# Attention inner order: a later values-and-sums block, earlier normalising, and Wo loaded in four pieces

## The chip, the cores and the metric

The kernel runs on one core of one Trainium2 chip. The metric is the device time in microseconds, the median of the runs; lower is better.

## The reference

A gated cross-attention block (16 batches, 100 queries, 361 keys, width 512, 16 query heads in 4 groups that share keys and values) followed by a gated feed-forward block with weights quantised to three levels and activations to 8 bits.

```python
scores = einsum('bqghd,bkgd->bghqk', Q / sqrt(dh), K) + m * rel   # ALiBi slope times distance
scores = where(mask, scores, neg)
w = softmax(scores, axis=-1)
out = einsum('bghqk,bkgd->bqghd', w, V).reshape(b, q_len, 512)
return out @ Wo
...
x = x + tanh(g_xattn) * xattn(layernorm(x), ctx, ctx, mask, Wq, Wk, Wv, Wo)
x = x + tanh(g_ffn) * ffn(layernorm(x))      # silu(bit_linear) * bit_linear, rms_norm, bit_linear
```

## The kernel before

The program is written engine by engine, with its own semaphores: each engine's order is the order of its code. There are four stages: normalising x and projecting Q (kept in a scratch in DRAM), projecting K and V of the 16 batches, attention, and the feed-forward block over 12 full tiles of 128 rows and a tail. POOL quantises the feed-forward weights (24 pieces of 1024 columns, L526 to L538) during attention, each piece waiting for the loads that free its place; ring buffers of queries and keys (`qs`, `ks`, four slots) are filled from DRAM by SP.

Attention runs in steps b; one step works on three batches at once. A step on PE has eight slots u. Slot u begins with `scores(b, u)` (L1340): the plain scores of two heads of batch b, written to `wide[u % 2]`, from which DVE takes the row maxima (`largest_scores`, L1005). Behind them comes what the table `BEHIND[u]` lists, each entry with how many batches it lags:

- `("t", lag, j)`: `scores_t`, block j of 12 of the transposed scores (L1354), to `bank[j % 2]`; ACT takes its exponential into `p_t` (L718). Block 0 needs the batch's stored maxima (`nm_in`).
- `("pv", lag, kt)`: `values_and_sums`, one of three blocks (L1364, L1367): four matmuls of values and four of row sums, twice four rows of the trace, into `bank[2]` and `bank[3]`. After the third, ACT copies both out (`keep_pv`: `sum_kept` L731, `o_t` L732), and the next batch's first block waits for that.
- `("turn", ...)`: the maxima of the last batch are turned (L1373), copied by ACT to `nm_t` (L724, in the trace under its helper's line L631), and stored by SP into the rows of `qs` (`store_max`, L391). Slot 1's scores wait for the copy.

`scores(b, u)` also waits for the maxima of two slots before (u - 2), since they share a buffer. So slot 3 waits for the maxima of slot 1, slot 6 for those of slot 4, and slot 0 of the next step for those of slot 6.

The sums of a batch are inverted by ACT (`log_sums` L739, `inverse_sums` L744) in the step after the copy, between the exponentials of blocks 5 and 6. DVE refines the inverse and multiplies (`normalise(b - 3, step)`, steps 0, 1 and 2: L1021, L1024, L1029). The table `NORMALISE_BEHIND` says behind which slot's maxima each of them stands.

Wo is 1 MB. SP loads it (L432), ACT copies it at reduced precision to `wo_h` (L811, under L631 in the trace) behind step 9, and DVE forms `wo_l` (L1062) behind step 10. It is used after the last step. SP's order within a step is: `store_max(b - 1)`, then `load_qk(b + 2)` (L399, L401, L406) once transposed block 11 of batch b - 2 is done, then Wo.

Of the kernel before, what the change touches and what calls it, by code (L numbers as in the profile page):

```python
# [36 lines left out]
B, SQ, D = 16, 100, 512  # L37
# [3 lines left out]
G, HPG, DH = 4, 4, 32  # L41
# [33 lines left out]
QUANT_BYTES = QCH * 2  # L75


NORMALISE_BEHIND = {3: (0, 1), 5: (2,)}
O_TILES = (2, 3, 4, B)
BEHIND = {0: [("t", 2, 4), ("t", 2, 5), ("pv", 2, 0), ("turn", 1, 0), ("t", 2, 6), ("t", 2, 7)],  # L80
          1: [("t", 2, 8)],
          2: [("t", 2, 9), ("t", 2, 10)],
          3: [("t", 2, 11), ("pv", 2, 1)],
          4: [("t", 1, 0)],
          5: [("t", 1, 1), ("t", 1, 2), ("pv", 2, 2)],
          6: [("t", 1, 3)],
          7: []}


def flamingo_block(nc, x, ctx_t, mask, gates, wq, wk, wv, wo, w_ffn, ln_w, alibi_q, alibi_k, eye, out):  # L90
# [143 lines left out]
    with ctx:  # L234
# [3 lines left out]
        def sem(name):  # L238
            return ctx.enter_context(nc.semaphore(name))
# [9 lines left out]
        wo_in = sem("wo_in")  # L249
# [94 lines left out]
        def _(sp):  # L344
# [42 lines left out]
            def store_max(b):  # L387

                sp.wait_ge(nm_ready, b + 1)
                for part in range(2):  # L390
                    sp.dma_start(qs[b % SLOTS][ROWS_S + part:ROWS_S + part + 1, :, :].bitcast(F32).rearrange("p g (h q) -> p (g h) q", h=HPG),  # L391
                                 nm_t[H * part:H * part + H, :].bitcast(F32)).then_inc(nm_in, 16)

            def load_qk(b):

                slot = b % SLOTS
                q, n = q_scratch[b:b + 1], "o t (d g) n -> (o t d) g n"
                for rows, src in ((qs[slot][0:2 * DH], q), (qs[slot][2 * DH:3 * DH], q[:, 0:1])):
                    sp.dma_start(rows.bitcast(F32), src.rearrange(n, g=G)).then_inc(qk_in[slot], 16)  # L399
                for third, part in enumerate((0, 0, 1)):  # L400
                    sp.dma_start(ks[slot][DH * third:DH * (third + 1)].bitcast(F32),  # L401
                                 k_all[:, b, part, :].bitcast(F32)).then_inc(qk_in[slot], 16)
                if b == LATE_SLOT:
                    store_max(1)
                    sp.wait_ge(late_set, 2)
                sp.dma_start(ks[slot][100:101, :, 0:SK].bitcast(F32),  # L406
                             m_scratch[b:b + 1].rearrange("(o g) n -> o g n", g=1).broadcast_to([1, G, SK])).then_inc(qk_in[slot], 16)
# [13 lines left out]
            def attention_step(b):  # L421
                if b == 1:
                    store_max(0)
                    sp.wait_ge(kl_ready, B)
                    load_qk(LATE_SLOT)
                elif b > 2:
                    store_max(b - 1)
                if 2 <= b < B - 2:
                    sp.wait_ge(st_done, (b - 1) * UNITS)
                    load_qk(b + 2)  # L430
                if b == 8:
                    sp.dma_start(wo_f[:, :, :], wo).then_inc(wo_in, 16)  # L432

            def load_xb(t, par, rows=P):
                if not (isinstance(t, int) and t < 2):
# [193 lines left out]
        def _(act):  # L629
# [82 lines left out]
            def exps(b, *units):  # L712

                for j in units:
                    act.wait_ge(st_done, b * UNITS + (j + 1))
                    if j % G == 0 and b > 0:
                        act.wait_ge(pv_done, b * 3 - (2 - j // G))
                    nc.scalar.activation(p_t[:, j, :], bank[j % 2][0:KT, 0:HQ], ACT.Exp).then_inc(exp_done, 1)  # L718
# [16 lines left out]
            def log_sums(b):  # L735
                act.wait_ge(o_copied, b * 2 + 1)
                if not (isinstance(b, int) and b == 0):
                    act.wait_ge(o_ready, b)
                nc.scalar.activation(log_sum[:, :], sum_kept[:, :], ACT.Ln).then_inc(log_ready, 1)  # L739
# [38 lines left out]
            def attention_step(b):  # L778
                if b >= 2:
                    exps(b - 2, 4, 5)  # L780
                if b >= 3:
                    log_sums(b - 3)
                    inverse_sums(b - 3)
                if 2 <= b <= B:
                    turned_max(b - 1)
                if b == B + 1:
                    xq_round(0)
                if b >= 2:
                    exps(b - 2, 6, 7)
                if b == B:  # L790
                    o_high(1)
                if b == B + 1:
                    first_out()
                if b >= 2:
                    exps(b - 2, 8, 9, 10, 11)
                if b <= B:
                    exps(b - 1, 0, 1, 2)
                if 2 <= b <= B:
                    keep_pv(b - 2)
                if b <= B:  # L800
                    exps(b - 1, 3)

            for b in range(B):
                ctx_step(b)
# [2 lines left out]
            for b in range(1, STEPS):  # L807
                attention_step(b)
                if b == 9:
                    act.wait_ge(wo_in, 16)  # L810
                    copy_high(wo_h[:, :, :], wo_f[:, :, :]).then_inc(wo_high, 1)  # L811
                if b == B - 2:
                    act.wait_ge(wo_low, 1)
                    o_high(0)
# [87 lines left out]
        def _(dve):  # L902
# [150 lines left out]
            for b in range(2, B):  # L1053
                for u in range(PAIRS):
                    largest_scores(b, u)
                    if b >= 3:
                        for step in NORMALISE_BEHIND.get(u, ()):
                            normalise(b - 3, step)
# [529 lines left out]
```

## Time and profile before

| | |
|---|---|
| median of 3 runs | 531.79 us (531.22 to 534.74) |
| the profiled execution | 530.64 us |
| its span, first to last instruction | 528.8 us |
| PE busy, DVE busy, ACT busy, POOL busy | 89%, 70%, 62%, 44% of the span |
| chain that ended last, by engine | PE 51%, ACT 14%, DVE 14%, DMA 11%, issue 6% |
| step 2 of attention begins | 153.15 us |
| step 15 of attention begins | 312.61 us |
| mean granted TensorE clock | 0.982 |

The share of busy time is an average over stages. A matmul's end is modelled and matmuls overlap, so the distance between starts says more than their durations. A row of windows has the stretch, its length, the busy time and count of instructions of PE, PE's weight loads, DVE, ACT and POOL, the granted clock (1.00 is 2.4 GHz), the DMA engines' busy share and GB/s. The chain that ended last is followed back from the last instruction to what released each piece of work.

### The profile page before, as it was taken

How to read it: one execution, taken by the hardware profiler on the slowest of the kernel's cores; microseconds unless marked ns; L12 is line 12 of the kernel's file. 1: busy time of each engine (PE TensorE's matmuls, PEld its weight loads, DVE VectorE, ACT ScalarE, POOL GpSimd, SP SyncE). 2: the span in 40 equal slices, each digit the busy share in tenths (PEclk: the TensorE clock that was granted, in tenths of full speed). 3: DMA queues.
4: the chain of work that ended last, by engine and by line, in shares of the span. 5: the costliest groups of instructions: out<-in, count | busy, mean ns of one | idle time of the engine just before them, and what ended most of it. 6: DMA issues, size and time to landing. Idle time of an engine off the chain costs nothing.

```text
span 528.8 us, 8322 instructions
## 1 busy us (share of the span) xinstructions
PE 472.7 (89%) x2854; PEld 296.5 (56%) x2854; DVE 368.5 (70%) x674; ACT 327.9 (62%) x560; POOL 232.8 (44%) x250
## 2 busy tenths in 40 slices
PE   1799979998989999988889999888999999999965
PEld 1699979987954444443444445434454555555522
DVE  4876634466646888885698785387777777777762
ACT  2366637566336666664766776667777777777760
POOL 1000000000156677855263680147777677777630
PEclk9999999999979999998999999999999999999998
DMA  7889897999548788879667730112534333333323
GB/s 196 244 276 401 323 363 251 245 349 283 151 89 205 177 191 196 198 156 246 146 135 169 161 107 32 71 31 40 135 86 91 89 89 89 89 90 89 70 51 70
DMA packets 62402, 85.51 MB, mean 162 GB/s; under 512 B 37314, under 2 KB 48786, under 8 KB 60446
## 3 DMA queue, kind: packets, MB, share of 16 engines
q1 hardware_dynamic: 57182, 59.87, 44.5%
q0 software_dynamic: 3456, 12.58, 8.8%
q10 hardware_dynamic: 1728, 12.58, 6.8%
q8 instruction: 21, 0.34, 0.3%
q14 instruction: 15, 0.12, 0.1%
HBM read 57.94 MB, written 9.85 MB: 128 GB/s over the span
## 4 chain that ended last, share of the span: by engine, by line
PE 51%; ACT 14%; DVE 14%; DMA 11%; issue 6%; SPq 2%; POOL 1%; ACTq 0%; POOLq 0%; DVEq 0%
PE bank L1364 7%; DMA ct<-ctx_t 6%; PE bank L1354 6%; PE wide L1340 6%; PE wide L1271 6%; PE bank L1367 6%; PE wide L1440 5%; PE bank L1271 5%; PE bank L1312 5%; PE bank L1450 3%; ACT p_t L718 3%; DVE row_max L1005 3%; ACT sq_junk L832 2%; ACT act L822 2%; DMA qs<-nm_t 2%
## 5 line engine op out<-in xcount | busy, mean ns | idle before, releaser
L1005 DVE TENSOR_REDUCE row_max<-wide 100x2 f32<-100x722 f32 x128 | 110.4, 902 | 36.4 <-PE wide L1340 36.2
L718 ACT ACTIVATE p_t<-bank 121x400 f32<-121x400 f32 x192 | 92.4, 503 | 52.5 <-PE bank L1354 48.7
L1440 PE MATMUL wide<-w_q,xq 128*128 128x512 bf16 x384 | 86.8, 380 | 2.7 <-DVE h L1122 2.4
L572 POOL TENSOR_TENSOR z<-h,lnw 128x512 f32<-128x512 f32 x48 | 61.0, 1272 | 15.3 <-DVE h L1122 14.7
L1440 PEld LDWEIGHTS wide<-w_q,xq 128*128 128x128 bf16 x384 | 35.5, 98 | 51.6 <-DVE h L1122 7.9
L526 POOL DMA_DIRECT2D quant_in<-w_ffn x24 | 14.3, 595 | 99.5 <-PE bank L1312 93.0
L1340 PE MATMUL wide<-ks,qs 101*100 101x362 f32 x192 | 49.6, 346 | 9.0 <-DVE row_max L1005 5.2
L1354 PE MATMUL bank<-qs,ks 103*121 103x400 f32 x144 | 51.1, 386 | 6.1 <-DMA qs<-nm_t 2.5
L1312 PE MATMUL bank<-wv_f,ct 128*121 128x128 f32 x384 | 46.2, 278 | 4.3 <-DMA ct<-ctx_t 4.3
L952 DVE TENSOR_TENSOR ctl<-ct,cth 128x1445 fp32r<-128x1445 f32 x16 | 26.6, 1664 | 31.8 <-ACT cth L631 31.8
L1312 PEld LDWEIGHTS bank<-wv_f,ct 128*121 128x121 f32 x384 | 45.4, 189 | 4.9 <-DMA ct<-ctx_t 4.9
L840 ACT ACTIVATE z<-z,small 128x1024 f32<-128x1024 f32 x24 | 29.6, 1235 | 29.4 <-DVE small L1156 29.4
L1450 PE MATMUL bank<-w_q,yq 128*128 128x512 bf16 x192 | 45.3, 390 | 2.3 <-DMA yq<-y_int 2.3
L538 POOL TENSOR_SCALAR w_q<-quant_in 128x1024 bf16<-128x1024 f32 x24 | 31.9, 1329 | 34.4 <-DMA ks<-m_scratch 26.8
L1340 PEld LDWEIGHTS wide<-ks,qs 101*100 101x100 f32 x192 | 28.5, 168 | 29.2 <-issue 16.9
L1122 DVE TENSOR_TENSOR h<-act,wide 128x512 f32<-128x512 f32 x50 | 34.2, 685 | 13.8 <-ACT act L822 13.5
L1364 PE MATMUL bank<-p_t,v_all 120*32 120x400 f32 (+1 forms) x384 | 43.6, 526 | 0.0
L1367 PE MATMUL bank<-p_t,ones_keys 120*32 120x400 f32 (+1 forms) x384 | 42.2, 512 | 0.0
L822 ACT ACTIVATE act<-wide,small 128x512 f32<-128x512 f32 x50 | 33.6, 676 | 7.9 <-PE wide L1440 7.7
L1354 PEld LDWEIGHTS bank<-qs,ks 103*121 103x121 f32 x144 | 25.8, 188 | 18.1 <-ACT p_t L718 11.7
L531 POOL TENSOR_SCALAR quant_in<-quant_in,small 128x1024 f32<-128x1024 f32 x24 | 28.4, 1184 | 16.6 <-DMA quant_in<-w_ffn 14.3
L1450 PEld LDWEIGHTS bank<-w_q,yq 128*128 128x128 bf16 x192 | 18.7, 99 | 26.9 <-DMA yq<-y_int 4.3
(157 smaller groups left out, 919.3 us busy)
## 6 DMA issues: line engine op xcount, KB each, us to landing
quant_in<-w_ffn POOLq DMA_DIRECT2D x24, 512.0 KB, 5.7
ct<-ctx_t SPq DMA_DIRECT2D x16, 722.0 KB, 10.3
ks<-k_all SPq DMA_DIRECT2D x36, 181.0 KB
q_scratch<-qhl SPq DMA_DIRECT2D x16, 400.0 KB, 7.5
abs_a<-w_ffn ACTq DMA_DIRECT2D x6, 1024.0 KB, 7.2
abs_b<-w_ffn ACTq DMA_DIRECT2D x6, 1024.0 KB, 9.0
qs<-q_scratch SPq DMA_DIRECT2D x12, 400.0 KB
xb<-x SPq DMA_DIRECT2D x12, 256.0 KB, 2.9
```

What stands on the lines that cost most here:

```text
L572: nc.gpsimd.tensor_tensor(z[par][0:rows, c], h[0:rows, c], lnw[0:rows, c], ALU.mult).then_inc(z_done, 1)
L718: nc.scalar.activation(p_t[:, j, :], bank[j % 2][0:KT, 0:HQ], ACT.Exp).then_inc(exp_done, 1)
L822: nc.scalar.activation(silu_g[j % 2][0:rows, :], wide[j % 2][0:rows, 0, :], ACT.Silu, scale=f_cg[par][0:rows]).then_inc(silu_done, 1)
L1005: nc.vector.tensor_reduce(row_max[b % 2][:, 2 * u:2 * u + 2], wide[u % 2][0:SQ, :, 0:SK], AX_X, ALU.max).then_inc(s_maxed, 1)
L1271: mm = nc.tensor.matmul(dst, a, b, start=(n == 0), stop=(n == last))
L1312: mm = nc.tensor.matmul(bank[2 + b % 2][0:KT, kt * P:(kt + 1) * P], tile[:, c * SK + k0:c * SK + k0 + KT], wv_f[:, c, :], start=(c == 0), ...
L1340: mm = nc.tensor.matmul(wide[u % 2][0:SQ, k, 0:SKP], qs[b % SLOTS][0:ROWS_S, g, h * SQ:(h + 1) * SQ], ks[b % SLOTS][0:ROWS_S, g, :], start ...
L1354: nc.tensor.matmul(bank[j % 2][0:KT, 0:HQ], ks[b % SLOTS][:, g, KT_AT[kt]:KT_AT[kt] + KT], qs[b % SLOTS][:, g, :], start=True, stop=True). ...
L1364: nc.tensor.matmul(bank[2][32 * g:32 * g + 32, 0:HQ], v_all[0:n, b, kt * P + DH * g:kt * P + DH * (g + 1)], p_t[0:n, kt * G + g, :], start ...
L1367: mm = nc.tensor.matmul(bank[3][32 * g:32 * g + 32, 0:HQ], ones_keys[0:n, :], p_t[0:n, kt * G + g, :], start=(kt == 0), stop=(kt == 2), ti ...
L1440: mm = nc.tensor.matmul(wide[j % 2][0:rows, m, :], xq[par][:, c, 0:rows], w_q[:, m * C + c, 512 * j:512 * j + 512], start=(c == 0), stop=( ...
L1450: mm = nc.tensor.matmul(bank[1][0:rows, :], yq[:, k, 0:rows], w_q[:, 2 * C + k // 4, (k % 4) * D:(k % 4 + 1) * D], start=(k == 0), stop=(k ...
```

## The change

Three things. The third values-and-sums block of batch b - 2 stands behind transposed block 3 in slot 6 and no longer behind block 2 in slot 5; ACT's copies of it stand behind four exponentials and not three. The normalising operations stand behind slots 0 and 3 instead of 3 and 5. Wo is loaded in four pieces of 256 KB, one in each of steps 5 to 8, instead of one megabyte in step 8.

```diff
-NORMALISE_BEHIND = {3: (0, 1), 5: (2,)}
+NORMALISE_BEHIND = {0: (0, 1), 3: (2,)}
...
-          5: [("t", 1, 1), ("t", 1, 2), ("pv", 2, 2)],
-          6: [("t", 1, 3)],
+          5: [("t", 1, 1), ("t", 1, 2)],
+          6: [("t", 1, 3), ("pv", 2, 2)],
...
-                if b == 8:
-                    sp.dma_start(wo_f[:, :, :], wo).then_inc(wo_in, 16)
+                if 5 <= b < 5 + HPG:
+                    sp.dma_start(wo_f[:, b - 5, :], wo[:, b - 5, :]).then_inc(wo_in, 16)
...
                 if b <= B:
-                    exps(b - 1, 0, 1, 2)
+                    exps(b - 1, 0, 1, 2, 3)
                 if 2 <= b <= B:
                     keep_pv(b - 2)
-                if b <= B:
-                    exps(b - 1, 3)
...
-                    act.wait_ge(wo_in, 16)
+                    act.wait_ge(wo_in, 16 * HPG)
```

PE from slot 5 of a middle step to the first scores of the next, before (`wide` is written by scores, `bank0` and `bank1` by transposed scores, `bank2` and `bank3` by values and sums):

```order
L1340 MATMUL wide1<-ks0_72,qs0_69 100x362 x2
L1354 MATMUL bank1<-qs_late_67,ks_late_68 121x400
L1354 MATMUL bank0<-qs_late_67,ks_late_68 121x400
L1364 MATMUL bank2<-p_t_75,v_all_55 32x400 x4
L1367 MATMUL bank3<-p_t_75,ones_keys_51 32x400 x4
L1340 MATMUL wide0<-ks0_72,qs0_69 100x362 x2
L1354 MATMUL bank1<-qs_late_67,ks_late_68 121x400
L1340 MATMUL wide1<-ks0_72,qs0_69 100x362 x2
L1340 MATMUL wide0<-ks1_73,qs1_70 100x362 x2
```

The same place on PE now (line numbers are two lower):

```order
L1338 MATMUL wide1<-ks0_72,qs0_69 100x362 x2
L1352 MATMUL bank1<-qs_late_67,ks_late_68 121x400
L1352 MATMUL bank0<-qs_late_67,ks_late_68 121x400
L1338 MATMUL wide0<-ks0_72,qs0_69 100x362 x2
L1352 MATMUL bank1<-qs_late_67,ks_late_68 121x400
L1362 MATMUL bank2<-p_t_75,v_all_55 32x400 x4
L1365 MATMUL bank3<-p_t_75,ones_keys_51 32x400 x4
L1338 MATMUL wide1<-ks0_72,qs0_69 100x362 x2
L1338 MATMUL wide0<-ks1_73,qs1_70 100x362 x2
```

The block has moved behind slot 6's scores and one transposed block; it stands ahead of slot 7's scores.

DVE in a middle step, from slot 0's maxima to the split of the maxima, before:

```order
L1005 TENSOR_REDUCE row_max_97<-wide 100x2 x4
L1021 TENSOR_TENSOR log_sum<-sum_kept,inv_sum 128x400
L1024 SCALAR_TENSOR_TENSOR log_sum<-log_sum,inv_sum 128x400
L1005 TENSOR_REDUCE row_max_97<-wide 100x2 x2
L1029 SCALAR_TENSOR_TENSOR o_t<-o_t,log_sum 128x4x100
L1005 TENSOR_REDUCE row_max_97<-wide 100x2 x2
L1012 TENSOR_SCALAR nm_q<-row_max_97 100x16
```

And now:

```order
L1003 TENSOR_REDUCE row_max_97<-wide 100x2
L1019 TENSOR_TENSOR log_sum<-sum_kept,inv_sum 128x400
L1022 SCALAR_TENSOR_TENSOR log_sum<-log_sum,inv_sum 128x400
L1003 TENSOR_REDUCE row_max_97<-wide 100x2 x3
L1027 SCALAR_TENSOR_TENSOR o_t<-o_t,log_sum 128x4x100
L1003 TENSOR_REDUCE row_max_97<-wide 100x2 x4
L1010 TENSOR_SCALAR nm_q<-row_max_97 100x16
```

The first two normalising operations stand ahead of the maxima of slots 1, 2 and 3, the third ahead of those of slots 4 and 5.

## Rows read from the trace of the kernel before

**Rows 1.** Windows of steps 3, 9, 10, 11, 12; columns as told above.

```profile
167.06:178.74 11.68, 10.90 (x78) 5.49 (x78) 9.34 (x14) 7.74 (x17) 7.35 (x7) 1.00 0.89 182
...
237.06:252.84 15.78, 12.59 (x78) 5.74 (x78) 9.44 (x14) 7.96 (x18) 7.81 (x7) 0.89 1.03 241
252.84:265.38 12.54, 11.10 (x77) 5.45 (x78) 8.71 (x14) 9.04 (x18) 3.81 (x4) 1.00 0.60 134
265.38:277.63 12.25, 11.20 (x77) 5.48 (x78) 11.45 (x15) 7.64 (x17) 9.03 (x8) 1.00 0.57 134
277.63:289.29 11.66, 10.88 (x78) 5.52 (x78) 9.81 (x14) 7.75 (x17) 4.36 (x5) 1.00 0.72 168
```

**Rows 2.** The chain that ended last, end of step 12: start us, us, what.

```profile
288.23 0.92 DVE row_max L1005
```

**Rows 3.** Timeline of PE, step 12: start us, us, work [idle before it].

```profile
278.47 0.88 PE L1364 MATMUL bank<-p_t,v_all 120*32 120x400 f32 x8
...
280.64 0.55 PE L1340 MATMUL wide<-ks,qs 101*100 101x362 f32 x2
...
282.33 0.49 PE L1340 MATMUL wide<-ks,qs 101*100 101x362 f32 x2
...
284.42 0.57 PE L1340 MATMUL wide<-ks,qs 101*100 101x362 f32 x2
284.83 0.35 PE L1354 MATMUL bank<-qs_late,ks_late 103*121 103x400 f32 x1
...
286.14 0.88 PE L1364 MATMUL bank<-p_t,v_all 121*32 121x400 f32 x8
...
287.62 0.58 PE L1340 MATMUL wide<-ks,qs 101*100 101x362 f32 x2
...
289.29 0.55 PE L1340 MATMUL wide<-ks,qs 101*100 101x362 f32 x2 [0.58 <-DVE row_max L1005]
```

**Rows 4.** The same stretch on ACT and DVE.

```profile
279.75 0.54 ACT L744 ACTIVATE inv_sum<-log_sum 128x400 f32<-128x400 f32 x1
...
281.23 2.54 DVE L1005 TENSOR_REDUCE row_max<-wide 100x2 f32<-100x722 f32 x3 [1.69 <-PE wide L1340]
...
287.75 0.51 ACT L731 ACTIVATE sum_kept<-bank 128x400 f32<-128x400 f32 x1 [1.01 <-PE bank L1367]
```

**Rows 5.** Timeline of steps 8 to 10, then the low clock's stretch as in rows 1.

```profile
235.00 0.52 SPq L432 DMA_DIRECT2D wo_f<-wo  x1
239.95 1.23 SPq L391 DMA_DIRECT2D qs<-nm_t  x2
...
246.91 0.44 PE L1354 MATMUL bank<-qs,ks 103*121 103x400 f32 x1 [2.48 <-DMA qs<-nm_t]
...
252.49 1.93 ACT L631 ACTIVATE wo_h<-wo_f 128x2048 fp32r<-128x2048 f32 x1
...
256.47 0.54 PE L1340 MATMUL wide<-ks,qs 101*100 101x362 f32 x2 [0.66 <-ACT nm_t L631]
...
247.48:250.89 3.41, 3.41 (x20) 0.95 (x18) 1.39 (x2) 1.42 (x3) 2.50 (x2) 0.50 1.06 181
```

**Rows 6.** Timeline of DVE, start of step 11.

```profile
266.39 2.29 DVE L1062 TENSOR_TENSOR wo_l<-wo_f,wo_h 128x2048 fp32r<-128x2048 f32 x1
```

**Rows 7.** The first two normalising operations from 160 to 330 us: ns min/median/max.

```profile
L1021 DVE TENSOR_TENSOR log_sum<-sum_kept,inv_sum x13: 564/566/1040, 173.1 to 318.7; 128x400 f32<-128x400 f32 x13
L1024 DVE SCALAR_TENSOR_TENSOR log_sum<-log_sum,inv_sum x13: 574/1292/1378, 173.7 to 319.3; 128x400 f32<-128x400 f32 x13
```

**Rows 8.** The maxima's stores, issue to landing: at 193 us, at 240, all 28 after 160.

```profile
DMA to landing us min/median/max: 3.0/3.3/3.5
...
DMA to landing us min/median/max: 5.6/5.9/6.3
...
DMA to landing us min/median/max: 1.7/2.7/6.3
```

**Rows 9.** Timeline of POOL, step 12.

```profile
281.20 1.05 POOL L538 TENSOR_SCALAR w_q<-quant_in 128x1024 bf16<-128x1024 f32 x1 [3.22 <-DMA ks<-m_scratch]
```

## The prediction

> **What bounds the kernel now.** On the page I read first the share of each engine on the chain that ended last (PE 51%, the table above), then, since the change touches the attention loop alone, I cut the trace at the start of each step's first score matmul [rows 1]. An undisturbed step takes 11.66 us, give or take 0.02: steps 3 to 8 and 12 to 14, nine in all, of which the third and the twelfth stand there. Step 9 takes 15.78, step 10 12.54 and step 11 12.25, together 5.6 us more. So there are two questions: what holds the 11.66, and what made three long steps.
>
> In step 12 PE's row is nearly full. It stops for 0.58 us at one place: the first scores of step 13 wait for DVE's maxima of slot 6, and those could start only after the scores of slot 6, which the third values-and-sums block had held back [rows 2, 3]. The chain says the same: 0.92 us of DVE stand between the scores of slot 6 and the next step [rows 2]. DVE itself waits 1.69 us before slot 1's maxima [rows 4].
>
> In step 9 the 1 MB load of Wo is issued at 235.00, the two stores of the turned maxima behind it at 239.95; they land 5.6 to 6.3 us after issue, those of step 5 after 3.0 to 3.5, and PE waits 2.48 us for them [rows 5, 8]. From 247.48 to 250.89 the granted clock is 0.50, the 1.2 GHz level, after a stretch in which PE had stood still [rows 5]. Steps 10 and 11 hold ACT's copy of Wo (1.93 us) and DVE's subtraction for it (2.29 us) [rows 5, 6].
>
> **The change, part by part.** Times without a date are counted from the start of a step (277.63 for step 12).
>
> *1. Wo's load in four pieces.* The same bytes go out behind steps 5 to 8, 256 KB each. Three more issues of about half a microsecond stand on SP, each behind the loads of its step and ahead of the maxima's stores, which wait for ACT anyway: SP is free from about 235.5 to 239.95 [rows 5], so these issues cost nothing. Without the megabyte step 9 falls by 15.78 - 11.66 = 4.1 us, clock loss included. Of step 10's excess of 0.88, 0.62 is ACT's (slot 1's scores at 256.47 - 252.84 = 3.63 instead of 280.64 - 277.63 = 3.01 [rows 3, 5]); the other 0.26 I put down to loads that were late from step 9. **Gain 4.4.** Against it, each piece now stands ahead of one step's maxima. In step 9 the queues were full (DMA share 1.03) at 241 GB/s [rows 1]: a piece takes 1.1 us. The maxima of step 5 were issued at 2.9 and 3.5 and landed by about 7.0; PE wants them at 284.83 - 277.63 = 7.20 [rows 3], so that step has 0.2 of room. Others have more: the median of the 28 stores is 2.7 to landing, which leaves 1.0 [rows 8]. I take one step that loses 0.8 and two that lose 0.2: **-1.2**, with bounds 0 and 4 x 0.9 = 3.6.
>
> The trace holds one load of Wo, the megabyte, and so nothing on small against large. The Trainium skill ("DMA: Bandwidth & Descriptors", Measured, for loads on GpSimd's path) speaks against splitting: 64 KB reached 138 GB/s and 1 MB 341. As an estimate from that page a piece takes 0.8 to 1.9 us, and with the upper figure this term would be about -3.
>
> *2. The third block from slot 5 to slot 6.* Written out for the steady state: slot 4's scores start at 6.79, its maxima 0.61 later (as 288.23 after 287.62) and end at 8.30; a signal takes 0.15, so slot 6's scores start at 8.45. From there the row is now the same as behind slot 3: scores, one transposed block, one values block, 2.09 us (282.33 to 284.42). The block, 1.48 of it (286.14 to 287.62), starts at 9.06 and slot 7's scores at 10.54, and the next step's first 0.41 later (the gap of 284.42 to 284.83), at 10.95. Slot 6's maxima end at 10.0, under the block [rows 2, 3]. That is 0.71 less than 11.66. What is late next: ACT's two copies out of the block's banks. They start 1.61 after the block (287.75 - 286.14) and take 0.90 [rows 4], so they end 0.6 into the next step, and its first values-and-sums block wants them at 0.84 (278.47): covered by 0.2, less a signal. The exponential they used to hold up stands ahead of them now.
>
> *3. Normalising from slots 3 and 5 to slots 0 and 3.* The first operation waits for ACT's inverse, which ends at 279.75 + 0.54, 2.66 into the step [rows 4]. Undisturbed, the two take 0.57 each and a signal [rows 7], to 3.88; slot 1's maxima could start at 3.60 [rows 4]. So those end at 4.83, and slot 3's scores, which need them, move from 4.70 (282.33) to 4.98: **-0.28 a step**. In exchange slot 4's maxima start on time, as term 2 has assumed. Net 0.43 a step, which becomes 11.23; over steps 3 to 14 that is 5.2, and step 2, which normalises nothing, gives the whole 0.7. **Gain 5.9.** Behind step 15 I find 0.1 to 0.2 on either side (ACT's copies reach further into the last step, its fourth exponential comes sooner) and count nothing.
>
> *4. Wo's copy and subtraction have less cover.* The copy now follows the two bank copies, so it starts 0.5 into step 10 and not, as at 252.49, before it. The next exponential would be ready at 0.77 and starts at 2.3; the 1.5 reach slot 1's scores through the inverse and the turned maxima. Before they were 0.62: **-0.9.** The subtraction starts at 1.45 of step 11 and ends at 3.74. Slot 0's maxima, two normalising operations and slot 1's maxima queue behind it, so slot 3's scores come at 6.64 instead of 4.98: 1.66, against 12.25 - 11.66 = 0.59 before [rows 1, 6]. **-1.1.**
>
> *5. DVE against POOL.* The second normalising operation took 0.57 at least and 1.29 in the median, the first 0.56 to 1.04 [rows 7], and they are long where POOL quantises. The new place is 2.71 to 3.88. In step 12 POOL starts at 281.20, 3.57 into the step, on a load's landing [rows 9]; the loads go out at the same slot of a shorter step, so they land later in the next. I take two steps that lose 0.6. The third operation, at 6.5, falls where POOL is at work, and slot 4's maxima behind it start late; I take 0.2 in five steps. **-2.2**, with bounds 0 and rival C's.
>
> The Trainium skill ("SBUF — State Buffer", Who interferes with whom) says that a DVE operation with two SBUF inputs and a GpSimd operation that reads SBUF exclude each other for the whole instruction, the first to issue winning. The stretched rows fit an exclusion, though not always in that order: most first operations kept their 0.57 near a running POOL. If it held strictly, a meeting would cost up to the whole 1.05 of a POOL operation and the term about double.
>
> **Sum**: 4.4 - 1.2 + 5.9 - 0.9 - 1.1 - 2.2 = **4.9 us gained**. The profiled execution took 530.64 (1.8 of it outside its span), 1.15 under the median of 531.79. It would become 525.7 and the median **526.9**. Half the way to the bounds of terms 1 and 5 gives 525 to 529 for this case.
>
> **Rivals.**
> A, the forecast: 0.50.
> B, the covers hold: the pieces fit into the margin and POOL stays away, 4.9 + 3.4 = 8.3 gained, 523.5. For it: the room of most landings, and that POOL's operations mostly begin after the new place. 0.22.
> C, slower: **the normalising pair meets POOL in every step**. It then takes what it took in step 12, 1.04 + 1.30 and a signal, 2.37; slot 1's maxima start at 5.1, slot 3's scores come at 6.18, 1.20 later than in term 3. A step takes 12.43, 0.77 more than now: 12 x 0.77 = 9.2 lost, 0.7 and 4.4 won, 2.0 lost to term 4, in sum 6.1 slower, 537.9. The loop turns from gain to loss where the pair averages over 1.6. For it: 11 of 13 second operations were stretched in the old place. Against it: the new one lies before POOL's start. 0.05.
> D, the maxima still wait: the late landing is the queue's, not the megabyte's, and each of steps 6 to 9 loses 0.9 and the clock may fall once; 2.8 more lost, 529.7. 0.15.
> E, the block's move gives nothing, since slot 6's scores or the block wait for maxima or exponentials that I have put just in time: 5.9 not won, term 5 hidden in those waits, 530.6. 0.08.
>
> In A's own tail: step 11 will have PE waits of about 1.0 and 1.2 close together, and step 9's wait was followed by the low clock. From the late block's start to step 10 it took 252.84 - 246.91 = 5.9, where step 12 took 289.29 - 284.83 = 4.5; so 1.5 us if it falls.
>
> **Numbers.** A measurement of this kernel can tell some 1% (5.3 us) from no change. Faster by more means under 526.5: all of B and 0.4 of A, 0.42. Slower by more: C, 0.05. Within: 0.53. The range 523.2 to 530.6 leaves out C, half of E and the edges of B and D.
>
> **What the new profile would show.** If right: steps of about 11.2, steps 10 and 11 near 12.8; no PE wait before a step's first scores but one of 0.3 before slot 3's; the maxima landing within some 4 us everywhere and no low clock near 247; ACT's copy of the sums at the very end of a step. If wrong: steps of 11.6 (term 2), PE waiting for slot 1's maxima over 0.5 in most steps (C), PE waiting for the stored maxima in steps 6 to 9 (D). Term 5 is the weakest, since POOL's place within a step hangs on when its loads land.

## Result and profile after

The changed kernel takes **539.47 us** (median of 4 runs, 536.91 to 550.19); the kernel before took 532.51 beside it (4 runs, 531.22 to 534.74). The ratio is 1.0116, with a 95% interval of 1.0064 to 1.0167: slower, by little more than a measurement can tell, where 526.9 was forecast. Two later comparisons, each on one chip, gave 0.9971 [0.9930, 1.0011] and 1.0089 [1.0050, 1.0128]. Every ratio leaves out runs more than 1.5% above the fastest of their kernel; of the changed kernel these had a mean granted clock of 0.950 to 0.968, the others 0.958 to 0.981, so the ratios tell rather too little of a loss by the clock.

The profiled execution took 537.54 us against 530.64. First the windows of steps 3 to 6 and 9 to 11 of the changed kernel, then two stretches inside steps 10 and 11 (columns as in [rows 1]):

```profile
169.25:182.55 13.30, 11.06 (x79) 5.46 (x78) 8.89 (x13) 7.86 (x18) 8.43 (x8) 1.00 0.99 200
182.55:196.53 13.98, 12.49 (x79) 6.00 (x78) 10.38 (x13) 7.85 (x18) 10.98 (x12) 0.88 0.64 170
196.53:207.55 11.02, 10.81 (x79) 5.45 (x78) 8.71 (x13) 7.85 (x18) 6.48 (x7) 1.00 0.86 200
207.55:219.95 12.40, 11.01 (x78) 5.52 (x78) 10.36 (x13) 7.88 (x18) 9.81 (x10) 1.00 0.84 196
...
242.10:253.81 11.71, 11.07 (x79) 5.46 (x79) 8.89 (x13) 7.86 (x18) 7.45 (x8) 1.00 0.99 219
253.81:268.16 14.35, 12.88 (x78) 6.14 (x77) 8.94 (x13) 9.37 (x19) 4.05 (x5) 0.88 0.73 165
268.16:283.74 15.58, 13.63 (x78) 6.71 (x78) 11.04 (x14) 7.62 (x18) 9.76 (x8) 0.78 0.59 131
...
260.26:263.67 3.41, 3.41 (x19) 1.30 (x19) 2.13 (x3) 0.84 (x2) 1.18 (x2) 0.50 0.69 217
273.91:280.74 6.83, 6.05 (x26) 3.10 (x27) 3.98 (x6) 1.55 (x4) 6.23 (x6) 0.50 0.76 194
```

Read downwards: an undisturbed step (5) takes 11.02 where it took 11.66, and step 9 takes 11.71 where it took 15.78. Those are the gains. Against them steps 3, 4, 6, 10 and 11 are 1.4 to 4.6 above 11.02. In two of the long ones, and in step 4, the mean granted clock is below 1; the last two rows show it at 0.50, the 1.2 GHz level, for 3.4 and 6.8 us. In the loop it is there for 13.7 us, and was for 3.4 before (247.48 to 250.89).

PE's timeline of the changed kernel, at its waits:

```profile
178.72 0.44 PE L1352 MATMUL bank<-qs,ks 103*121 103x400 f32 x1 [2.04 <-DMA qs<-nm_t]
...
188.68 0.93 PE L1338 MATMUL wide<-ks,qs 101*100 101x362 f32 x2 [1.29 <-DVE row_max L1003]
...
258.28 0.54 PE L1338 MATMUL wide<-ks,qs 101*100 101x362 f32 x2 [0.78 <-ACT nm_t L631]
...
272.76 0.57 PE L1338 MATMUL wide<-ks_late,qs_late 101*100 101x362 f32 x2 [0.83 <-DVE row_max L1003]
...
274.69 0.93 PE L1338 MATMUL wide<-ks_late,qs_late 101*100 101x362 f32 x2 [0.99 <-DVE row_max L1003]
...
323.84 0.57 PE L1338 MATMUL wide<-ks_late,qs_late 101*100 101x362 f32 x2 [1.04 <-DVE row_max L1003]
```

The first is the stored maxima in step 3, the next slot 3's scores in step 4; then slot 1's in step 10, slots 2 and 3's in step 11, and slot 3's in step 15. Slot 3's scores, at 4.70 in an undisturbed step, come at 6.13, 6.07, 6.43, 6.53, 5.40 and 6.02 of steps 4, 6, 10, 11, 12 and 15. The pair of scores that begins at 188.68 takes 0.93 where such a pair takes 0.57: the clock has just gone to 0.50.

Why slot 3 was late in step 4, on DVE and POOL of the changed kernel:

```profile
184.94 1.11 POOL L531 TENSOR_SCALAR quant_in<-quant_in,small 128x1024 f32<-128x1024 f32 x1 [1.72 <-DMA quant_in<-w_ffn]
185.21 1.27 DVE L1019 TENSOR_TENSOR log_sum<-sum_kept,inv_sum 128x400 f32<-128x400 f32 x1 [0.31 <-ACT inv_sum L744]
186.14 1.24 POOL L533 TENSOR_SCALAR quant_in<-quant_in 128x1024 f32<-128x1024 f32 x1
186.51 1.29 DVE L1022 SCALAR_TENSOR_TENSOR log_sum<-log_sum,inv_sum 128x400 f32<-128x400 f32 x1
187.46 1.25 POOL L538 TENSOR_SCALAR w_q<-quant_in 128x1024 bf16<-128x1024 f32 x1
187.73 1.71 DVE L1003 TENSOR_REDUCE row_max<-wide 100x2 f32<-100x722 f32 x2
```

Both normalising operations take 1.3 beside POOL's quantising, not 0.57, and slot 1's maxima, which slot 3's scores need, start at 5.18 of the step instead of 3.74. In the kernel before, the same stretching cost nothing: the second operation took 1.29 or more in every undisturbed step, and slot 6's scores, which wait for the maxima behind it, were held back longer by the third block anyway.

In steps 6 and 14 something else came first. DVE's split of the maxima into two parts, which takes 0.17 alone, ran beside POOL at the start of the step and made the pair start 0.49 and 0.31 late:

```profile
208.69 1.04 DVE L1010 TENSOR_SCALAR nm_q<-row_max 100x16 fp32r<-100x16 f32 x1
307.63 0.86 DVE L1010 TENSOR_SCALAR nm_q<-row_max 100x16 fp32r<-100x16 f32 x1
```

Why it was late in step 11, on DVE:

```profile
269.61 2.28 DVE L1060 TENSOR_TENSOR wo_l<-wo_f,wo_h 128x2048 fp32r<-128x2048 f32 x1
271.81 0.90 DVE L1003 TENSOR_REDUCE row_max<-wide 100x2 f32<-100x722 f32 x1
272.63 0.58 DVE L1019 TENSOR_TENSOR log_sum<-sum_kept,inv_sum 128x400 f32<-128x400 f32 x1
273.25 0.57 DVE L1022 SCALAR_TENSOR_TENSOR log_sum<-log_sum,inv_sum 128x400 f32<-128x400 f32 x1
273.74 1.72 DVE L1003 TENSOR_REDUCE row_max<-wide 100x2 f32<-100x722 f32 x2
```

Here the queue is as forecast: subtraction, slot 0's maxima, the pair, slot 1's maxima.

The 6.9 us between the two profiles divide so. The loop (steps 3 to 14) has 3.0, 148.57 against 145.55; step 2 gives 0.7 back; behind step 15's start, up to the first gate matmul, 1.2 (33.50 against 32.28, with slot 3's wait of step 15); the rest 0.5 and 0.3. The other 2.6 lie before the first Q projection (20.77 against 18.15), where ACT waits longer for the load of Wq. The change touches nothing there, and that start lay anywhere from 18.1 to 22.3 in the profiles of all the kernels. So one profile against one profile overstates the change by as much; the ratios of many runs don't.

### The profile page after: what moved, and what is told of

Read it like the earlier page. It is cut to its first block, busy times and chain, and to the rows that moved or that the text cites. A ratio compares the mean times of both kernels' runs of the same rounds, so it can differ in the third digit from the quotient of the medians.

```text
span 535.7 us, 8311 instructions
## 1 busy us (share of the span) xinstructions
PE 478.2 (89%) x2840; PEld 300.4 (56%) x2854; DVE 364.7 (68%) x674; ACT 328.7 (61%) x560; POOL 229.1 (43%) x250
## 4 chain that ended last, share of the span: by engine, by line
PE 51%; DVE 15%; ACT 12%; DMA 12%; issue 6%; SPq 2%; POOL 0%; ACTq 0%; POOLq 0%; DVEq 0%
PE wide L1438 7%; PE wide L1338 6%; PE bank L1269 6%; DMA ct<-ctx_t 6%; PE bank L1362 6%; PE wide L1269 6%; PE bank L1352 5%; PE bank L1365 5%; PE bank L1310 5%; PE bank L1448 4%; ACT p_t L718 3%; DVE row_max L1003 3%; DMA qs<-nm_t 2%; DMA wq_f<-wq 2%; DMA yq<-y_int 2%
## 5 line engine op out<-in xcount | busy, mean ns | idle before, releaser
L1438 PE MATMUL wide<-w_q,xq 128*128 128x512 bf16 x372 | 85.3, 380 | 3.6 <-DVE h L1120 2.6
L1310 PE MATMUL bank<-wv_f,ct 128*121 128x128 f32 x384 | 47.6, 283 | 3.2 <-DMA ct<-ctx_t 3.2
L1310 PEld LDWEIGHTS bank<-wv_f,ct 128*121 128x121 f32 x384 | 47.1, 195 | 3.5 <-DMA ct<-ctx_t 3.5
L538 POOL TENSOR_SCALAR w_q<-quant_in 128x1024 bf16<-128x1024 f32 x24 | 29.5, 1228 | 41.6 <-DMA ks<-m_scratch 32.1
L1362 PE MATMUL bank<-p_t,v_all 120*32 120x400 f32 (+1 forms) x384 | 44.9, 541 | 0.8 <-ACT o_t L732 0.8
L1120 DVE TENSOR_TENSOR h<-act,wide 128x512 f32<-128x512 f32 x50 | 34.2, 685 | 14.0 <-ACT act L820 13.6
L1365 PE MATMUL bank<-p_t,ones_keys 120*32 120x400 f32 (+1 forms) x384 | 43.3, 524 | 0.0
L1352 PEld LDWEIGHTS bank<-qs,ks 103*121 103x121 f32 x144 | 26.5, 192 | 18.1 <-ACT p_t L718 12.1
```

The costliest lines, as they stand in the source:

```text
L1120: nc.vector.tensor_tensor(h[r, 512 * j:512 * j + 512], silu_g[j % 2][r, :], wide[j % 2][r, 1, :], ALU.mult).then_inc(h_done, 1)
L1310: mm = nc.tensor.matmul(bank[2 + b % 2][0:KT, kt * P:(kt + 1) * P], tile[:, c * SK + k0:c * SK + k0 + KT], wv_f[:, c, :], start=(c == 0), ...
L1352: nc.tensor.matmul(bank[j % 2][0:KT, 0:HQ], ks[b % SLOTS][:, g, KT_AT[kt]:KT_AT[kt] + KT], qs[b % SLOTS][:, g, :], start=True, stop=True). ...
L1362: nc.tensor.matmul(bank[2][32 * g:32 * g + 32, 0:HQ], v_all[0:n, b, kt * P + DH * g:kt * P + DH * (g + 1)], p_t[0:n, kt * G + g, :], start ...
L1365: mm = nc.tensor.matmul(bank[3][32 * g:32 * g + 32, 0:HQ], ones_keys[0:n, :], p_t[0:n, kt * G + g, :], start=(kt == 0), stop=(kt == 2), ti ...
L1438: mm = nc.tensor.matmul(wide[j % 2][0:rows, m, :], xq[par][:, c, 0:rows], w_q[:, m * C + c, 512 * j:512 * j + 512], start=(c == 0), stop=( ...
```

## Experiments

"Loop" is the length of steps 3 to 14 in the one profiled execution. A time is the median of all runs of the kernel (6 to 13); a ratio, with its 95% interval, is to the kernel before on the same chip. The kernels came in four groups of four; the kernel before had medians of 535.19, 534.53, 534.16 and 533.30 beside them.

### Pieces alone, order alone

The kernel before with the four pieces (and ACT's wait for them):

```diff
+                if 5 <= b < 5 + HPG:
+                    sp.dma_start(wo_f[:, b - 5, :], wo[:, b - 5, :]).then_inc(wo_in, 16)
```

> Wo's load in four pieces, order as before. Theory T1 (the change loses where PE waits for slot 1's maxima at slot 3 and around Wo's copy and subtraction, and where the granted clock falls behind those waits; the pieces themselves are good): 4 us faster than before, step 9 at 11.7, step 10 at 12.3 with ACT's copy still before it, step 11 at 12.3, no half clock in steps 9 to 11. Rival T2 (the pieces delay the stored maxima and cost what the order wins): within 1 us of before, steps 6 to 9 each 0.5 to 1.5 longer than 11.66.

531.72 us, **0.9947** [0.9913, 0.9981]; loop 141.3. Steps 9, 10 and 11:

```profile
240.82:252.49 11.67, 10.91 (x77) 5.53 (x78) 10.06 (x14) 7.99 (x18) 6.74 (x7) 1.00 0.88 201
252.49:264.71 12.22, 10.84 (x78) 5.51 (x78) 9.42 (x14) 9.05 (x18) 4.14 (x4) 1.00 0.70 143
264.71:276.95 12.24, 11.20 (x78) 5.49 (x78) 11.63 (x15) 7.64 (x17) 6.42 (x6) 1.00 0.72 150
```

Step 9 is an ordinary step, with no wait for stored maxima and no fall of the clock. The gain of term 1 is there, and no piece cost a step more than 0.2 (step 5, 11.85).

The changed kernel with the one megabyte in step 8 (and ACT's wait for it):

```diff
-                if 5 <= b < 5 + HPG:
+                if b == 8:
+                    sp.dma_start(wo_f[:, :, :], wo).then_inc(wo_in, 16)
```

> The new order with Wo as one megabyte in step 8. T1: about 4 us slower than the changed kernel, near 542 to 544, since step 9 has its stall back, and steps 4, 6, 10, 11 have the same long waits. T2: faster than the changed kernel in steps 6 to 9 in sum, and at least as fast over all.

540.54 us, **1.0106** [1.0067, 1.0145]. The loss is there without the pieces: it is in the order. That the megabyte costs 4 us on top of it, as expected, is not shown, since the changed kernel itself had 1.0116, 0.9971 and 1.0089. In the profile step 9 takes 14.65, with a wait of 1.84 for stored maxima.

### Early normalising undone, or alone

The changed kernel with the old places of normalising:

```diff
-NORMALISE_BEHIND = {0: (0, 1), 3: (2,)}
+NORMALISE_BEHIND = {3: (0, 1), 5: (2,)}
```

> The changed kernel with normalising back behind slots 3 and 5: block in slot 6 and pieces stay. T1: the waits at slot 3 go in every step, step 11 loses about 1.5 and no clock falls in steps 4 and 6, but slot 6's scores wait for slot 4's maxima, which stand behind the first two normalising operations (7.9 to 8.8, so 8.95 instead of 8.5): steps near 11.5, in sum 530 to 534. Rival T3 (the block in slot 6 is what hurts, through ACT's late copies and the transposed blocks behind them): as slow as the changed kernel, steps 4, 6, 10 and 11 unchanged.

529.81 us, **0.9901** [0.9866, 0.9936]; loop 141.6, steps 4 to 9 at 11.35 to 11.55, slot 3's scores at 4.64 in them. As expected, slot 6's scores now wait 0.3 to 0.45 for slot 4's maxima, so the block's move alone shortens a step by 0.1 to 0.3 and not by 0.64. Steps 10 and 11:

```profile
252.71:266.06 13.35, 11.31 (x79) 5.67 (x79) 9.81 (x13) 9.39 (x19) 4.02 (x4) 1.00 0.66 139
266.06:278.48 12.42, 11.23 (x78) 5.48 (x77) 11.60 (x14) 7.74 (x18) 7.38 (x8) 1.00 0.63 141
```

Both are shorter than in the changed kernel, at full clock. Later the changed kernel and this one ran again side by side:

> The changed kernel beside the next three on one chip. T1: 0.997 to 1.012 of before; in its profile again at least two stretches of low clock between steps 9 and 11, and at least three steps whose slot 3 comes later than 5.4.

> The changed kernel with normalising back behind slots 3 and 5. T1: 0.5 to 1.5% faster than the changed kernel on this chip, no low clock between steps 3 and 14, steps of 11.4.

536.56 us, **1.0089** [1.0050, 1.0128], and 529.54 us, **0.9922** [0.9886, 0.9958]: one line of the program takes it from slower to faster. The second profile is not what was expected, though: its loop takes 148.8, longer than the changed kernel's beside it (143.6), and the clock is low for 3.4 us in each of steps 3, 5 and 10. It shows what the block's move leaves behind, and that one profile doesn't stand for a kernel's median. Steps 3 and 4, and PE in step 3:

```profile
168.29:183.60 15.31, 12.53 (x79) 5.84 (x78) 9.31 (x13) 7.85 (x18) 10.03 (x10) 0.89 0.96 213
183.60:195.26 11.66, 10.99 (x79) 5.54 (x78) 10.33 (x13) 7.91 (x18) 10.21 (x12) 1.00 0.64 164
```

```profile
178.18 0.45 PE L1352 MATMUL bank<-qs,ks 103*121 103x400 f32 x1 [2.58 <-DMA qs<-nm_t]
```

PE waits 2.58 for stored maxima in a step with no load of Wo, and 2.33 in step 5.

The early places alone, with the pieces, and the block in slot 5 as before; the edit against the kernel with the pieces alone:

```diff
-NORMALISE_BEHIND = {3: (0, 1), 5: (2,)}
+NORMALISE_BEHIND = {0: (0, 1), 3: (2,)}
```

> Wo in four pieces and normalising behind slots 0 and 3, with the third block left in slot 5 and ACT's copies where they were. T1: undisturbed steps of about 11.7 to 11.9 (the 0.58 before the next step is back, slot 3 waits 0.1 to 0.3), the same meetings with POOL at slot 3, step 11 near 13.5, step 10 at 12.2 since ACT's copy is before it again; in sum slower than the changed kernel or as slow. Rival T3 (the block is what hurts): faster than the changed kernel by 0.5% or more.

540.94 us, **1.0110** [1.0051, 1.0168], where the pieces alone had 0.9947. An undisturbed step takes 11.8, slot 3's scores come at 4.75, and at 5.4 to 5.6 in steps 3, 6, 10, 12, 13 and 15. Step 11:

```profile
271.93:288.35 16.42, 13.78 (x77) 6.73 (x78) 11.71 (x15) 7.53 (x17) 8.29 (x8) 0.79 0.72 158
```

PE hardly waits for stored maxima in it (0.2 in all, as with the pieces alone). So those waits go with the block in slot 6, and the loss with the early normalising: without it 0.9947 and 0.9901 or 0.9922 (block in slot 5, in slot 6), with it 1.0110 and 0.9971 to 1.0116.

### POOL's part

The changed kernel, with the first two of POOL's three quantising operations on 8 columns only; the rest of that quantisation is left out:

```diff
-nc.gpsimd.tensor_scalar(buf, buf, w_scale[:, n // 8:n // 8 + 1], ROUND
+nc.gpsimd.tensor_scalar(buf[:, 0:8], buf[:, 0:8], w_scale[:, n // 8:n // 8 + 1], ROUND
```

> The changed kernel, with the first two of POOL's three quantising operations on 8 columns instead of 1024 (this part of the weight quantisation is left out); loads, waits and the third operation stay. T1, contention of the early normalising with POOL's operations: the long slot 3 (6.1 instead of 4.70 us into the step) goes in most of steps 4, 6, 12 and 15, the half clock of step 4 with it; about 3 us faster than the changed kernel, near 535 to 537. Rival (the late slot 3 comes from ACT's inverse or the loads, not from POOL): the same steps stay at 12.4 and 14.0 and the time within 1 us of the changed kernel's.

535.19 us, **0.9927** [0.9871, 0.9983], which rests on 4 of its 12 runs; by the medians of all it is 1.001, so no gain over the whole is shown, where 3 us were expected. Loop 144.5. Steps 4, 6 and 10:

```profile
181.36:192.76 11.40, 11.07 (x80) 5.46 (x78) 8.89 (x13) 7.87 (x18) 4.13 (x7) 1.00 0.94 211
203.79:214.80 11.01, 10.81 (x78) 5.50 (x78) 8.71 (x13) 7.85 (x18) 4.13 (x6) 1.00 0.93 180
249.46:264.52 15.06, 12.89 (x79) 5.90 (x79) 9.57 (x13) 9.39 (x19) 2.12 (x4) 0.89 0.68 144
```

Steps 4 and 6, 13.98 and 12.40 in the changed kernel, are down and slot 3's scores are at 4.70 from step 3 to 9. One profile would be little proof, for the changed kernel's third has 4.70 in steps 4 and 6 too (and late scores in 5, 7 and 9). But all eighteen profiles say the same of POOL: an operation of the pair that ran beside none of POOL's never took over 0.58 in steps 3 to 14, and every one over 0.68 ran beside one for most of its time. Slot 3 stays late in steps 12 and 15 (5.44 and 5.66), against expectation: there the pair meets POOL's third operation, which is still whole. Steps 10 and 11 stay at 15.06 and 15.60. There are two costs.

### Wo's copies in quarters

The changed kernel, with ACT's copy in quarters behind steps 9 to 12 and DVE's subtraction behind 10 to 13:

```diff
-                if b == 9:
+                if 9 <= b < 9 + HPG:
                     act.wait_ge(wo_in, 16 * HPG)
-                    copy_high(wo_h[:, :, :], wo_f[:, :, :]).then_inc(wo_high, 1)
+                    copy_high(wo_h[:, b - 9, :], wo_f[:, b - 9, :]).then_inc(wo_high, 1)
...
-                if b == 10:
-                    dve.wait_ge(wo_high, 1)
+                if 10 <= b < 10 + HPG:
+                    dve.wait_ge(wo_high, b - 9)
```

> The changed kernel with ACT's copy of Wo cut into quarters behind steps 9 to 12 and DVE's subtraction into quarters behind steps 10 to 13, 0.5 and 0.6 us each. T1: no wait of a microsecond in steps 10 and 11 and no half clock there; steps 10 to 13 at 11.0 to 11.8 instead of 14.4, 15.6, 11.7, 11.0, so 6 us faster than the changed kernel, near 532 or a little under before. T2 or T3: 1 to 2 us faster at most.

> The changed kernel with Wo's copy and subtraction in quarters once more, since its first profile was disturbed: T1: 0.983 to 0.992 of before, no wait over 0.6 us before slots 1 to 3 of steps 10 to 13 except where POOL meets the normalising, 2 to 4 us faster than the filler kernel, since the waits themselves are gone too.

528.75 us, **0.9860** [0.9809, 0.9912], and 530.67 us, **0.9922** [0.9882, 0.9961]. Steps 10 and 11 of the second:

```profile
256.73:268.04 11.31, 10.81 (x79) 5.51 (x78) 8.71 (x13) 8.10 (x19) 3.82 (x4) 1.00 0.68 149
268.04:279.39 11.35, 10.86 (x79) 5.51 (x77) 9.31 (x14) 8.12 (x19) 5.48 (x6) 1.00 0.70 153
```

11.31 and 11.35 instead of 14.35 and 15.58, so a quarter costs its step about 0.3. The long steps move elsewhere in part: both profiles have low clock in the loop for 6.8 us (step 5 of the second takes 15.18, with slot 3's scores at 6.11).

Both cures together, the quarters and POOL's small operations:

> The changed kernel with Wo's copy and subtraction in quarters and the first two of POOL's three operations on 8 columns (that part of the weight quantisation is left out). If the two account for the loss, steps 3 to 14 sum to 134 to 136 (12 of 11.02 and about 0.3 more in steps 10 to 13), there is no low clock among them, and the time is 1.5 to 2% under before. If a third cost is left, the sum stays above 138.

529.90 us, **0.9899** [0.9844, 0.9954]; loop 142.2 and not 134 to 136. Nearly all steps take 11.0 to 12.3, but step 9 doesn't:

```profile
237.72:253.60 15.88, 12.67 (x78) 5.92 (x77) 8.89 (x13) 8.14 (x19) 2.55 (x6) 0.89 1.04 196
```

```profile
248.16 0.44 PE L1352 MATMUL bank<-qs,ks 103*121 103x400 f32 x1 [3.00 <-DMA qs<-nm_t]
```

The third cost: stored maxima that land late, and the low clock behind it (from 250.1).

### The clock

Is the low clock in steps 10 and 11 a cost of its own? The changed kernel with 14 unused matmuls in PE's waits, which change no result (they hold up slot 1's scores of step 10 by 0.3):

```diff
+            FILL = {(10, 1): 6, (11, 2): 4, (11, 3): 4}
...
+                    for _ in range(FILL.get((b, u), 0)):
+                        nc.tensor.matmul(bank[3][:, 400:512], ones_all[:, :], ident[:, 0:112], start=False, stop=False)
                     scores(b, u)
```

> The changed kernel with 14 extra matmuls of 112 columns, whose result nobody uses, in PE's waits of steps 10 (6) and 11 (4 and 4). If the low clock behind those waits is what makes steps 10 and 11 3.3 and 4.6 us longer than 11.02, they become about 12.7 and 13.0, with no half clock there, and the whole 2 to 3 us faster in spite of more work. If the waits themselves are the loss, steps 10 and 11 stay at 14.4 and 15.6 or grow.

531.09 us, **0.9927** [0.9889, 0.9965]. Slot 3's scores come at 6.59 and 6.54, as late as without the matmuls (6.43 and 6.53), yet the steps take 12.91 and 12.86. Then beside the changed kernel on one chip, with the same 14 matmuls at other places as a control:

> The changed kernel unaltered, on the same chip as the next three, since the first filler run (0.993 of before) and the changed kernel (1.012) were timed on different ones. Theory T1 (waits, and the low clock behind them): 1.007 to 1.016 of before, low clock in steps 10 and 11 again. Rival (the first measurement was that chip's): within 0.5% of before.

> The 14 unused matmuls in the waits of steps 10 and 11 once more, for the same chip. T1 with the clock as the larger part: 4 us (steps 10 and 11: 29.9 to 25.8) to 10 us faster than the changed kernel in these rounds; if steps 10 and 11 alone differ, 4.

```diff
-            FILL = {(10, 1): 6, (11, 2): 4, (11, 3): 4}
+            FILL = {(10, 5): 6, (11, 5): 4, (11, 6): 4}
```

> The same 14 matmuls ahead of scores where PE does not wait: slots 5 of steps 10 and 11 and slot 6 of step 11. If it is the filled wait that keeps the clock, this is 1 to 3 us slower than the changed kernel, with the low clock in steps 10 and 11 as there. Rival (extra matmuls help wherever they stand): as fast as the filler in the waits.

533.92, 531.40 and 538.49 us; **0.9971** [0.9930, 1.0011], **0.9987** [0.9941, 1.0032], **0.9997** [0.9941, 1.0053], on 8 of 12, 9 of 12 and 5 of 13 runs. The 4 to 10 us expected of the filled waits are not in the ratios, and the control can't be told from the changed kernel by them. Steps 10 and 11 of the changed kernel:

```profile
254.72:270.92 16.20, 13.81 (x79) 6.66 (x78) 10.12 (x13) 9.39 (x19) 4.02 (x4) 0.79 0.59 126
270.92:285.37 14.45, 12.49 (x79) 5.87 (x78) 10.94 (x14) 7.75 (x18) 10.29 (x8) 0.88 0.54 122
sum 30.65, PE 26.30 PEld 12.53 DVE 21.06 ACT 17.14 POOL 14.31; mean PE 13.15 PEld 6.26 DVE 10.53 ACT 8.57 POOL 7.15
```

and with the matmuls in the waits:

```profile
248.99:262.31 13.32, 12.41 (x90) 7.06 (x90) 9.43 (x13) 9.36 (x19) 5.00 (x4) 1.00 0.67 145
262.31:275.87 13.56, 12.62 (x95) 7.50 (x94) 11.53 (x14) 7.75 (x18) 8.18 (x8) 1.00 0.57 132
sum 26.88, PE 25.02 PEld 14.55 DVE 20.96 ACT 17.11 POOL 13.18; mean PE 12.51 PEld 7.28 DVE 10.48 ACT 8.56 POOL 6.59
```

PE in step 11 of the latter (its line numbers past the edit are a few higher):

```profile
267.69 1.04 PE L1403 MATMUL bank<-ident,ones_all 128*128 128x112 f32 x8
269.55 0.57 PE L1338 MATMUL wide<-ks_late,qs_late 101*100 101x362 f32 x2 [0.82 <-DVE row_max L1003]
```

Slot 3's scores wait for the same maxima, at 7.24 of the step even later than in the changed kernel (6.54), and still the two steps take 3.8 less. In the control they take 17.33 and 18.33, at a granted clock of 0.80 and 0.81; its profiled execution was the slowest of its 13 (553.73), so only the clock's fall is to be read from it. All three profiles of the changed kernel have the low clock in both steps, both with filled waits in neither. So within the two steps the clock's part is shown: 3.8 here, and 29.93 - 25.77 = 4.2 between the first profiles. Over the whole kernel the three ratios don't differ by more than their intervals; the medians of all runs, 0.9996, 0.9948 and 1.0081, stand further apart, but have no interval. The low clock comes at other places too (202.5 and 246.9 in this profile of the changed kernel).

The mean granted clock of every run gives an estimate over the whole. The traces have two levels, 0.50 and 1.00, so twice what is missing to 1, times the span, is the time at the lower. Its median is 34.2 us for the changed kernel beside 21.1 with the old normalising, on one chip (24.2 before), and 31.0 beside 24.4 with the filled waits, on the other occasion. Were TensorE the limit in all of that time, half of the difference would be lost: 6.6 of the 7.0 us between the first two medians, and 3.3 where the second two differ by 2.5. So the clock can be most of the loss, as an upper bound; how much of it is the waits' own isn't separated by this.

### Better versions

Old normalising with the quarters:

> Block in slot 6, normalising behind slots 3 and 5 as before, Wo's load in four pieces and its copy and subtraction in quarters. T1: steps of 11.4 throughout, since slot 3 never waits and POOL's meeting with the normalising costs only what slot 4 waits; faster than the kernel with old normalising and whole copies by 2 to 3 us, near 527. Rival (early normalising is worth more than its meetings with POOL cost): slower than the quarters kernel with normalising behind 0 and 3.

529.65 us, **0.9923** [0.9887, 0.9959], with the lowest loop of all, 138.7, and no low clock in it. The 2 to 3 us that it was to gain on whole copies (0.9901 and 0.9922) aren't there.

Normalising behind slots 1 and 4, with the quarters:

```diff
-NORMALISE_BEHIND = {0: (0, 1), 3: (2,)}
+NORMALISE_BEHIND = {1: (0, 1), 4: (2,)}
```

> As the one with quarters, but normalising behind slots 1 and 4. The pair then starts at about 4.5, after slot 1's maxima, so slot 3 has no wait and slot 4's scores wait for slot 2's maxima only if the pair is stretched by POOL. T1: undisturbed steps of 10.7 to 10.8, disturbed ones 11.2, all in all 3 to 5 us faster than with slots 3 and 5, near 523 to 525. Rival (a step is held by something else once slot 3 is free): no faster than with slots 3 and 5.

528.45 us, **0.9897** [0.9867, 0.9926], but by another way than expected: steps of 11.6 to 11.8, not 10.7. In eleven of the twelve steps slot 4's scores wait 0.2 to 0.5 for slot 2's maxima, which now stand behind the pair, stretched by POOL in most steps:

```profile
188.03 1.38 DVE L1022 SCALAR_TENSOR_TENSOR log_sum<-log_sum,inv_sum 128x400 f32<-128x400 f32 x1
190.28 0.58 PE L1338 MATMUL wide<-ks,qs 101*100 101x362 f32 x2 [0.41 <-DVE row_max L1003]
```

The rest of the 0.6 to 0.8 above 11.02 wasn't traced. What is left of the gain is that nothing is disturbed much (loop 140.7, no low clock, no step over 11.82).

All versions with the block in slot 6 and the old normalising, the quarters or both lie between 0.986 and 0.992 of the kernel before, and can't be told apart; the intervals of most overlap that of the pieces alone (0.9947) too.

## Why the prediction was wrong

**Right.** Step 9's gain of 4.1 (15.78 to 11.71, or 11.67 with the pieces alone). Terms 2 and 3 for an undisturbed step: it takes 11.02. It needs both moves, as the prediction said: 11.35 to 11.55 with the block's alone, 11.8 with the normalising's alone. The block's move with the pieces, without early normalising, is faster than before by 0.8 to 1.0% in two comparisons, of which the pieces alone have 0.5. The forecast of 11.23 was 0.21 too long: slot 1's maxima start at 3.74, by the records just before the pair ends at 3.82, so slot 3's scores stay at 4.70. Step 2's 0.7.

Against the sum of the prediction the loop is 7.2 too long in the profile (141.35 forecast: 145.55 less 4.1 + 0.3 + 5.2 - 1.2 - 0.9 - 1.1 - 2.2). The excess of each step over 11.02 says where, with 2.5 to the good from the 12 x 0.21 above.

**Term 4 failed, 4.7 of it.** Its waits were right: slot 1's scores of step 10 at 4.47 (forecast 3.63 + 0.9 = 4.53), slot 3's of step 11 at 6.53 (6.64). But steps 10 and 11 have 3.3 + 4.6 = 7.9 over an undisturbed step where the terms had 3.2. The rest is the clock. The prediction saw two PE waits close together, priced the low clock at 1.5 for step 11, and left it in "A's own tail", outside the sum and the rivals. It came in both steps, in each of the three profiles of the changed kernel: 3.4 us in one and 6.8 in the other. The price was right, the place at nothing was not: 1.5 for a fall of 3.4 us makes 4.5 for these 10.2, of the 4.7 missing. With PE kept busy in the same waits the steps took 12.91 and 12.86: "steps 10 and 11 near 12.8" is what a kernel without the clock's fall does. This is the main failure.

**Term 5 failed in size and place, 3.2.** It had two meetings of the pair with POOL at 0.6. The meetings were in steps 4, 6 and 12 (and 15, outside the loop), at 1.3 to 1.4 each but for 0.7 in step 12, and step 4's had the clock fall behind it; in steps 6 and 14 the split of the maxima met POOL, which the prediction did not have at all. The steps' excess: 2.96, 1.38, 0.71 and 0.31 (step 14), together 5.4 against 2.2. Rival C had the mechanism (slot 3's scores at 6.18, measured 6.13 and 6.07), but in every step; outside steps 10 and 11 slot 3 was late in two to four of the ten, which ones varying from run to run. So C's side of the result came out, though not through C alone: the early normalising put DVE's chain from the pair to slot 1's maxima to slot 3's scores on the path, with no room, and everything that delays it (POOL, Wo's subtraction, a late inverse) stops PE.

**Term 1's loss was under-sized, 1.9, and its cause was wrong.** Stored maxima landed late in step 3 (2.3 with what follows) and step 9 (0.7; step 8 has another 0.1). Step 3 has no piece of Wo ahead of it, and with the pieces and the old order there was no such wait. PE wants them where it did, at 7.27 of the step (7.20 before), and they are issued where they were; it is the landing that has moved, in step 3 from 7.05 to 9.43. Its two stores before, then in the changed kernel:

```profile
DMA to landing us min/median/max: 2.6/3.1/3.5
DMA to landing us min/median/max: 3.8/4.9/6.0
```

The DMA engines' busy share was 0.89 in that step and is 0.99. With the block in slot 5 and the pieces no store landed later than 7.3 in its step; with the block in slot 6 the latest of each profile came at 7.6 to 10.4. That is rival D in its effect, which the prediction tied to steps 6 to 9. It is shown so far: with the block in slot 6 and the pieces, PE waited 0.6 to 5.7 us for stored maxima in twelve of thirteen profiles (those of the control and of the order alone not counted), with the block in slot 5 and the pieces not over 0.2 in two. That a shorter step leaves the loads less time, and the stores a fuller queue, would explain it and is not shown; why they land late in one step and not in another is open.

**Costed at nothing, and nothing it was**: SP's three more issues; ACT's bank copies (PE waits 0.2 for them once). Not at nothing: the tail behind step 15, 1.2.

The Trainium skill ("TensorE: Matmul & The Clock Gate", A second HAM failure mode: psum-queue depth-cycling) says that frequent short idle times between groups of matmuls can make the clock swing between its levels. The trace agrees: in steps 10 and 11 the clock fell with no single wait over 1.0, and in step 4 at the end of one of 1.29. Had that section been set beside the two waits which the prediction had worked out, the fall would have been a rival.

What stays open: how much of the 1% is the clock and how much the waits themselves. The filled kernel settles it for two steps; for the whole there is only the estimate from the granted clocks. And by the ratios the loss is 1% in two comparisons and none in the third.

## What to carry to other kernels

Before an operation is moved earlier on its engine, see who waits for the one right behind it: here the early pair made an undisturbed step 0.3 to 0.5 shorter than the block's move alone did, and put its own stretching by POOL onto PE in the disturbed ones, which cost more. Price PE's waits of about 1 us that stand close together with the low clock behind them, not by their length, and divide what delays them; work of 2 us in quarters cost about 0.3 a step here, where the whole cost 3.3 and 4.6. Where a change shortens a step, look at the DMA with the least room: it may land later.

## What the runs showed of the hardware

- In the changed kernel the granted clock fell to 0.50 behind waits of 0.34, 0.78 and 0.19 us (step 10), and after one of 0.83 and within one of 0.99 (step 11), for 3.4 and 6.8 us. With fourteen small matmuls in such waits it stayed at 1.00 in these two steps, in both profiles that had them there, and not in the one with them elsewhere.
- One kernel's profiled executions differed in where it fell: the changed kernel's loop took 148.6, 150.0 and 143.6 us in three profiles.
- DVE's operation on two tiles of 128x400 took 1.27 beside POOL's instead of 0.57, and POOL's next, which fell between DVE's two, 1.24. The Trainium skill ("SBUF — State Buffer", Who interferes with whom) has the later one blocked for the whole of the other's instruction. By that the pair's operations, begun 0.84 and 0.87 before the end of a POOL operation, would take 1.41 and 1.44; they took 1.27 and 1.29, which nearly fits. The kernel before doesn't fit: in seven of thirteen steps the first operation kept its 0.57 although a POOL operation had begun 0.1 to 0.7 earlier and was still running (at 196.45 beside one begun at 195.76, which took 2.16, where such a one takes 1.04 alone).
- DVE's split of the maxima, one input of 100x16, took 1.04 and 0.86 beside POOL's operations and 0.17 without.
- A store of 6 KB landed 3.8 to 6.0 us after issue in step 3 of the changed kernel, in a step where the DMA engines' busy share was 0.99.
